# A four-layer graph network on one core: the first hop's chunks stay transposed from the join to the weights, the masked layer joins by products

## The chip, the cores and the metric

The kernel runs on one core of a Trainium2 chip. The metric is the device time of one execution in microseconds. Engines are named as the profile names them: PE (TensorE, with PEld for its weight loads), DVE (VectorE), ACT (ScalarE), POOL (GpSimd) and SP (SyncE, which issues most transfers).

## The reference, cut to what matters

`x` is 4096 x 64, `adj` 4096 x 4096, all float32. Four layers follow one another, each with a layer norm and a ReLU ahead and a residual sum behind. `norm_relu` below stands for those two steps.

```python
h = norm_relu(x)                                   # layer 0
x = x + 1.0 - 0.1 * h - 0.01 * sum(h * (adj @ h), axis=1)
h = norm_relu(x)                                   # layer 1: two hops
for k in range(2):
    h = tanh(concat([adj @ h, h], axis=1) @ W[k])
x = x + h
h = norm_relu(x)                                   # layer 2: weights by position
support = h @ weight
rank = cumsum(adj != 0, axis=1); deg = rank[:, -1:]
k = minimum(deg, 100); pos = rank - (deg - k)
x = x + where(adj != 0 and pos > 0, 0.5 ** (k - pos), 0) @ support + bias
h = norm_relu(x)                                   # layer 3
u = tanh(concat([h, t], axis=1) @ W1 + b1) @ W2 + b2
XB = h @ B.T
x = x + u + adj @ XB - sum(adj, axis=1) * XB
```

In a hop, `concat([adj @ h, h]) @ W` is computed as `adj @ (h @ Wtop) + h @ Wbottom`. The kernel keeps `h @ Wtop` in `X` as the next sweep's source and `h @ Wbottom` in `Z` until the sweep's sums are there.

## The kernel before

Five sweeps run over the whole adjacency: L0 (layer 0), L1A and L1B (the two hops), L2 (the masked layer) and L3. A sweep is 8 chunks of 512 result rows, a chunk is 16 blocks, and a block is two tiles of 128 source rows by 512 columns in float32. Two blocks, a pair of 1 MB, come with one transfer. Fifteen pairs stay in SBUF (`cache`). All others pass through six slots of `land`, in an order that turns round from sweep to sweep (L1A and L2 run backward over the chunks), so that the last six pairs of one sweep serve the next. Apart from the first chunk, a sweep loads six pairs a chunk, and seven in the one chunk that caches only one pair. SP issues the load of a slot (`load`, L714) when the instructions that read it are done: TensorE's block in all sweeps but L2, the mask on VectorE in L0 and L2 (L1116), the row totals on VectorE in L1A and L1B (L1085).

In L0, L1A, L1B and L3 a block is two products (L1320), one tile each, side by side in the two column halves of the array: 64 columns of weights (`X`), 512 columns of adjacency streaming. The two halves of the accumulator `accA` hold the sums of the even and the odd tiles, transposed (features on the partitions). So each chunk has an epilogue: ScalarE copies `accA` to `accS` (L821), and the *join* on TensorE (L1222) adds the two halves with a stacked identity, `wt("join")`. With `accS` as the weights the join also turns the chunk into rows: 4 x 2 products of 64 columns.

In L1A the epilogue goes on like this. `hop_added` on VectorE (L975) adds `Z`. ScalarE takes the tanh into `hS` (L833). The *turn* on TensorE (L1196, `transposed`) transposes four tiles, ScalarE copies them to `rowsT` (L801), and the *hop* (L1257) multiplies them with 128 columns of hop weights, which gives rows for `X` and `Z` (copied by L837). L0's epilogue ends with the same turn and hop. `rowsT` is also used, under the name `partS`, by the counting of L0's neighbours; the last step of that on VectorE is `left` (L1030), which raises `left_made`.

In L1B the tanh goes to `natS`, is added to the rows, normalized, turned and multiplied by the layer 2 weights (key 6, L1247). Its copy to `natS` is key 8 on ScalarE (L851), and GpSimd splits the result into high and low halves (`split_rows`).

In L2 the mask of a block is a step of VectorE (L1116), six blocks ahead of TensorE. TensorE multiplies the mask with a triangle (`triangle`, L1357), ScalarE turns the counts into weights (L564; in two blocks of a chunk, 3 and 13, VectorE does that, L562), and TensorE multiplies them with the rows, three blocks later (`weigh`, L1370). The result is a full 128-partition accumulator with a high and a low half of the features. Its join is four transposes of 128 x 128 (L1214), half in one block and half in the next, and VectorE adds both halves one after the other (L1054, L1057), centres the rows (L946, L947), forms the variance (L952, L953) of what GpSimd squared (L741), and after GpSimd's `pow` and scaling (L734, L744) writes the normalized rows (`norm_rows`, L965). TensorE transposes them (L1234) and multiplies them with `B.T` (L1244).

No scheduler orders the epilogues. Each engine runs through the same loop of blocks, and tables give the block behind which a step of an epilogue is put on each engine: `STAGES_L0`, `STAGES_L1A`, `STAGES_L1B`, `STAGES_L2` for a chunk's epilogue within the sweep, and `QUICK` for the last chunk's, which falls into the next sweep's chunk 0. An engine waits where it comes to a step whose input isn't there, and everything behind it on that engine waits too. On VectorE the keys of L2 count one higher than the step's number: key 4 is the sum and centring, 5 the variance, 6 the norm.

Of the kernel before, what the change touches and what calls it, by code (L numbers as in the profile page):

```python
# [17 lines left out]
D = 64  # L18
# [136 lines left out]
def copied_no(p, c, i=0):  # L155

    return {L0: c, L1B: 8 + 2 * c + i, L2: 24 + c, L3: 32 + c}[p]


def tr_no(p, c):  # L160

    return {L0: c, L1A: 8 + c, L1B: 16 + c, L2: 24 + c}[p]
# [91 lines left out]
def evac_no(c, b):  # L254
# [5 lines left out]
HT_PE = {L0: "turn", L1A: "turn", L1B: "turn", L2: 7}  # L260
HT_ACT = {L0: "turned", L1A: "turned", L1B: "turned", L2: 7}
# [6 lines left out]
STAGES_L1A = {1: 2, "added": 4, "tanh": 6, "turn": 8, "turned": 9, "hop": 11, "hopped": 13}  # L268
STAGES_L2 = {0: 2, "join0": 4, "join1": 5, 4: 5, 5: 7, 6: 9, 7: 13, 8: 15}
STAGES_L1B = {1: 3, "added": 5, "tanh": 6, 3: 7, 4: 8, 5: 10, "turn": 12, "turned": 13, 6: 15, 7: 15}  # L270
# [3 lines left out]
         L1B: {1: 1, "added": 2, "tanh": 3, "turn": 5, "turned": 5, "hop": 7, "hopped": 8},  # L274
         L2: {"tanh": 0, 4: 2, 5: 4, "turn": 8, "turned": 9, 6: 10, 7: 10, 8: 11,
# [15 lines left out]
LEFT_L1A = {"counts": 3, "weights": 4, "left": 6, "left out": 8}  # L291
# [3 lines left out]
def stages_after(p, c, b, before, before2):  # L295
# [12 lines left out]
    if p == L1B:  # L308
        found = at_block({8: 2}, before2) if before2 else []
        return found + at_block(STAGES_L1B, before) + at_block({"rows": ROWS_AT}, (p, c))  # L310
# [30 lines left out]
def gnn_kernel(nc, x_in, adj_in, left_in_d, wts_in, tri_in, out):  # L341
# [8 lines left out]
    with ExitStack() as ctx:  # L350
# [178 lines left out]
        def hop_out(i):  # L529
            return spare[:, 2:4, 0:2 * P].rearrange("p b (t y d) -> p y b t d", y=2, d=D)[:, i]  # L530
# [267 lines left out]
        def _(act):  # L798
# [4 lines left out]
            def epilogue(at, e):  # L803
# [25 lines left out]
                if at == "tanh":  # L829
# [3 lines left out]
                    nc.scalar.activation((hS if p == L1A else natS)[:, :], tS[:, :], ACT.Tanh).then_inc(tanh_done, 1)  # L833
                if at == "hopped":
                    act.wait_ge(hop_done, hop_no(p, c) + 1)
                    for of, to in ((0, X[1] if p == L0 else X[0]), (1, Z)):
                        nc.scalar.activation(chunk(to, ch(p, c)).rearrange("p (b t d) -> p b t d", b=2, d=D),  # L837
                                             hop_out(of), ACT.Copy).then_inc(hop_evac, 1)
                if at == HT_ACT.get(p, None):
# [4 lines left out]
                    if p in (L0, L1A):  # L844
                        act.wait_ge(left_made, min(c + 1, NC - 1) if p == L0 else NC)
# [84 lines left out]
        def _(dve):  # L930
# [36 lines left out]
            def epilogue(at, e):  # L967
# [64 lines left out]
                elif p in (L1B, L2):  # L1032
# [6 lines left out]
                    if at == 3:  # L1039
# [8 lines left out]
                        else:  # L1048
# [4 lines left out]
                            parts = nat_of(p, c).rearrange("p (t h d) -> p h t d", h=2, d=D)  # L1053
# [129 lines left out]
        def _(pe):  # L1183
# [22 lines left out]
            def epilogue(at, e):  # L1206
                p, c = e
                if p == L2 and at in ("join0", "join1") or p == L2 and c == NC - 1 and at == 1:
# [16 lines left out]
                if at == HT_PE.get(p, None):  # L1225

                    tr_free(tr_no(p, c))
                    if p == L1A:
                        pe.wait_ge(tanh_done, tanh_no(p, c) + 1)
                    else:  # L1230
                        pe.wait_ge(h_ready, row_no(p, c) + 1)
# [245 lines left out]
```

## Time and profile before

| | |
|---|---|
| median of 3 runs | 705.63 us (705.1 to 707.02) |
| the profiled execution | 706.86 us |
| its span | 705.1 us |
| TensorE busy | 668.3 us, 95% |
| weight loads busy | 266.6 us, 38% |
| VectorE busy | 467.3 us, 66% |
| ScalarE busy | 195.6 us, 28% |
| GpSimd busy | 113.6 us, 16% |
| HBM traffic | 366 GB/s over the span |
| the last chunk of L0, L1A, L1B is copied from accA at | 177.5, 304.0, 428.2 us |

A busy share is a mean over the five sweeps. TensorE's instructions are pipelined and overlap in the rows, so a row's busy time is longer than what the row costs: the distance between the starts of two rows is the cost. "x16" is the number of instructions in a row. What stands in brackets is how long the engine was idle before the row, and what ended that. A load's time to landing counts from its issue, so it grows with the queue ahead of it.

### The profile page before, as it was taken

Reading aid. Unit: us, or ns where it says so; the run is one execution under the profiler, and the core shown is the slowest. Engines: PE = TensorE matmul, PEld = TensorE weight load, DVE = VectorE, ACT = ScalarE, POOL = GpSimd, SP = SyncE. Lnnn points to the kernel's source line nnn. Section 1 sums busy time; section 2 is a strip of 40 time slices with the busy share of each in tenths; the row PEclk is TensorE's granted clock in tenths of the full one; section 3 lists DMA queues with packets and bytes.
Section 4 is the critical chain, followed back from the end, with each engine's and each line's share of the span. In section 5 each row is a group of like instructions: output and inputs, shape, how many; then the busy total and the mean of one; then the engine's idle time right before and its main releaser. Section 6 shows DMA issues by size and latency. Waiting matters only on the chain.

```text
span 705.1 us, 10672 instructions
## 1 busy us (share of the span) xinstructions
PE 668.3 (95%) x3920; PEld 266.6 (38%) x3920; DVE 467.3 (66%) x796; ACT 195.6 (28%) x304; POOL 113.6 (16%) x132
## 2 busy tenths in 40 slices
PE   3999999999999999999999997999999999999997
PEld 1423333333433333343443333444444433333332
DVE  7677667777899999876888778899988910000000
ACT  2101111011211111111110016888888821111110
POOL 5111011111200000001322222222222211211111
PEclk9999999999999999999999999999999999999999
DMA  9999999998699999859999985999999379999992
GB/s 356 422 413 413 416 412 413 419 415 330 212 347 391 423 421 420 367 206 399 419 417 418 415 349 192 350 381 403 415 412 410 131 243 350 420 415 412 420 416 88
DMA packets 45220, 258.64 MB, mean 367 GB/s; under 512 B 6320, under 2 KB 14256, under 8 KB 14960
## 3 DMA queue, kind: packets, MB, share of 16 engines
q1 hardware_dynamic: 39528, 252.85, 89.0%
q10 hardware_dynamic: 5640, 5.10, 2.2%
q8 instruction: 32, 0.52, 0.3%
q14 instruction: 20, 0.16, 0.1%
HBM read 253.33 MB, written 4.59 MB: 366 GB/s over the span
## 4 chain that ended last, share of the span: by engine, by line
PE 59%; DMA 20%; DVE 14%; issue 3%; POOL 2%; ACT 1%; SPq 1%; ACTq 0%; DVEq 0%
PE accA L1320 39%; DMA land<-adj_blocks 17%; PE work L1357 6%; PE accA L1370 6%; DVE uS L1085 5%; DVE uS L1116 3%; DMA cache<-adj_blocks 2%; PE work L1222 2%; PE work L1283 1%; POOL rstd L734 1%; PE work L1196 1%; DVE wS L562 1%; PE accA L1289 1%; PE work L1338 1%; PE work L1257 1%
## 5 line engine op out<-in xcount | busy, mean ns | idle before, releaser
L1320 PE MATMUL accA<-land,X 128*64 128x512 f32 x1568 | 376.1, 599 | 15.9 <-DVE X L1157 10.9
L1320 PEld LDWEIGHTS accA<-land,X 128*64 128x64 f32 x1568 | 106.1, 137 | 190.5 <-issue 157.9
L1116 DVE TENSOR_SCALAR uS<-land 128x1024 bf16<-128x1024 f32 (+1 forms) x196 | 135.2, 733 | 29.3 <-DMA land<-adj_blocks 28.3
L1085 DVE TENSOR_TENSOR uS<-uS,land 128x512 f32<-128x512 f32 x194 | 138.7, 715 | 10.5 <-DMA land<-adj_blocks 0.7
L1320 PE MATMUL accA<-cache,X 128*64 128x512 f32 x480 | 118.3, 597 | 2.9 <-ACT accS L821 2.9
L564 ACT ACTIVATE wS<-work 128x1024 uint16<-128x1024 f32 x114 | 109.0, 1035 | 14.5 <-PE work L1357 13.6
L741 POOL TENSOR_TENSOR hS<-tS 128x256 f32<-128x256 f32 x24 | 23.5, 978 | 397.6 <-DVE tS L947 397.6
L1071 DVE TENSOR_TENSOR zS<-uS,work 128x256 f32<-128x256 f32 x8 | 3.4, 421 | 122.7 <-PE work L1222 105.6
L1357 PE MATMUL work<-uS,triA 128*128 128x512 bf16 x256 | 76.0, 379 | 7.2 <-DVE wS L562 5.8
L1370 PE MATMUL accA<-wS,X 128*128 128x512 bf16 x256 | 75.8, 379 | 0.0
L821 ACT ACTIVATE accS<-accA 128x512 f32<-128x512 f32 x32 | 19.1, 596 | 155.1 <-PE accA L1320 151.6
L1320 PEld LDWEIGHTS accA<-cache,X 128*64 128x64 f32 x480 | 35.3, 138 | 63.1 <-issue 52.8
L1338 PE MATMUL work<-uS,later 128*64 128x512 bf16 x256 | 49.0, 379 | 0.0
L1116 DVE TENSOR_SCALAR uS<-cache 128x1024 bf16<-128x1024 f32 (+1 forms) x60 | 39.4, 686 | 8.0 <-DMA cache<-adj_blocks 7.8
L734 POOL TENSOR_TENSOR rstd<-var,power 128x4 f32<-128x4 f32 (+1 forms) x25 | 31.8, 1271 | 35.6 <-DVE var L953 35.6
L1370 PEld LDWEIGHTS accA<-wS,X 128*128 128x128 f16 x256 | 25.0, 98 | 30.0
L801 ACT ACTIVATE rowsT<-work 128x256 f32<-128x256 f32 x24 | 9.2, 384 | 95.4 <-PE work L1196 95.4
L1357 PEld LDWEIGHTS work<-uS,triA 128*128 128x128 bf16 x256 | 23.1, 97 | 33.4 <-issue 8.8
L1085 DVE TENSOR_TENSOR uS<-uS,cache 128x512 f32<-128x512 f32 x46 | 31.8, 691 | 2.6
L1338 PEld LDWEIGHTS work<-uS,later 128*64 128x64 bf16 x256 | 16.3, 110 | 35.6 <-issue 28.3
L965 DVE TENSOR_SCALAR hS<-tS 128x256 f32<-128x256 f32 x24 | 10.0, 416 | 27.9 <-POOL tS L744 27.9
L1222 PEld LDWEIGHTS work<-wts,accS 128*64 128x64 f32 x512 | 20.7, 138 | 17.7 <-issue 16.1
(94 smaller groups left out, 383.9 us busy)
## 6 DMA issues: line engine op xcount, KB each, us to landing
land<-adj_blocks SPq DMA_DIRECT2D x221, 1024.0 KB, 10.4
cache<-adj_blocks SPq DMA_DIRECT2D x15, 1024.0 KB, 16.6
xin<-x_rows ACTq DMA_DIRECT2D x16, 128.0 KB, 7.0
x_rows<-zS ACTq DMA_DIRECT2D x9, 128.0 KB, 7.3
out_rows<-zS ACTq DMA_DIRECT2D x8, 128.0 KB, 7.0
uS<-counts ACTq DMA_DIRECT2D x60, 4.0 KB
x_rows<-zS SPq DMA_DIRECT2D x7, 128.0 KB, 10.9
rows_transposed<-rowsT SPq DMA_DIRECT2D x7, 128.0 KB, 7.8
```

Source lines behind the costliest of these rows:

```text
L564: ops.activation(w, of, ACT.Relu).then_inc(w_ready, 1)
L734: nc.gpsimd.tensor_tensor(out[:, 0:ntile], of[:, 0:ntile], power[:, 0:ntile], ALU.pow)\
L741: nc.gpsimd.tensor_tensor(hS[:, :], tS[:, :], tS[:, :], ALU.mult).then_inc(rows_squared, 1)
L821: last = nc.scalar.activation(accS[:, :], accA[:, c % 2, :], ACT.Copy)
L965: nc.vector.tensor_scalar(to, tS[:, :], 0.0, float(np.sqrt(D)), ALU.max, ALU.mult).then_inc(h_ready, 1)
L1085: nc.vector.tensor_tensor(total, total, of[:, i * W:(i + 1) * W], ALU.add)\
L1116: nc.vector.tensor_scalar(masks(b)[0:rows, :], block_of(p, c, b)[0:rows, :], 0.0, None, ALU.not_equal)\
L1222: last = nc.tensor.matmul(nat[half, j * D:(j + 1) * D], accS[:, at:at + D], wt("join"), start=True, stop=True)
L1320: last = nc.tensor.matmul(accA[k * D:(k + 1) * D, c % 2, :], tile(X[p % 2], TQ * q + k), of[:, k * W:(k + 1) * W], start=(b == 0), stop=(b ...
L1338: last = nc.tensor.matmul(spare[k * D:(k + 1) * D, c % 2, :], later[:, NT - t:NT - t + D], masks(b)[:, k * W:(k + 1) * W], start=(b == 0), ...
L1357: last = nc.tensor.matmul(work[:, 2 * tri_pair(n) + k, :], triA[:, :], masks(b)[:, k * W:(k + 1) * W], start=True, stop=True)
L1370: last = nc.tensor.matmul(accA[:, c % 2, :], tile16(TQ * q + k), weights(n)[:, k * W:(k + 1) * W].bitcast(BF16), start=(b == 0 and k == 0) ...
```

## The change

In L0 the hop's product is made in two forms: rows for `X` as before, with the first 64 columns of the weights, and the part for `Z` transposed, by two products with 64 x 64 weights and 256 columns of `rowsT` streaming. In L1A the join streams `accS` through `wt("join")` in two products of 256 columns, which leaves the chunk transposed. `Z` is added in that form, the tanh writes `rowsT` directly, and the hop reads it. The steps `turn` and `turned` are gone from L1A. The tanh waits for the hop before it and for `left_made`, since `rowsT` is shared; the last steps of L0's counting run one block sooner (`LEFT_L1A`). In L1B the product is behind block 14 instead of 15 and its copy behind block 15 instead of block 2 of the chunk after. In L2 the join is four products with 64 columns of `wt("join")`, so that TensorE adds the halves, and VectorE has one addition instead of two. The norm is behind block 10 instead of 9, and for L1B's last chunk variance and norm are behind L2's blocks 0 and 2 instead of 2 and 4.

```diff
-STAGES_L1A = {1: 2, "added": 4, "tanh": 6, "turn": 8, "turned": 9, "hop": 11, "hopped": 13}
-STAGES_L2 = {0: 2, "join0": 4, "join1": 5, 4: 5, 5: 7, 6: 9, 7: 13, 8: 15}
-STAGES_L1B = {1: 3, "added": 5, "tanh": 6, 3: 7, 4: 8, 5: 10, "turn": 12, "turned": 13, 6: 15, 7: 15}
+STAGES_L1A = {1: 2, "added": 4, "tanh": 6, "hop": 8, "hopped": 10}
+STAGES_L2 = {0: 2, "join0": 4, "join1": 5, 4: 5, 5: 7, 6: 10, 7: 13, 8: 15}
+STAGES_L1B = {1: 3, "added": 5, "tanh": 6, 3: 7, 4: 8, 5: 10, "turn": 12, "turned": 13, 6: 14, 8: 15}
...
-         L1B: {1: 1, "added": 2, "tanh": 3, "turn": 5, "turned": 5, "hop": 7, "hopped": 8},
-         L2: {"tanh": 0, 4: 2, 5: 4, "turn": 8, "turned": 9, 6: 10, 7: 10, 8: 11,
+         L1B: {1: 1, "added": 2, "tanh": 3, "hop": 5, "hopped": 6},
+         L2: {"tanh": 0, 4: 0, 5: 2, "turn": 8, "turned": 9, 6: 10, 7: 10, 8: 11,
...
-LEFT_L1A = {"counts": 3, "weights": 4, "left": 6, "left out": 8}
+LEFT_L1A = {"counts": 2, "weights": 3, "left": 5, "left out": 7}
...
-        found = at_block({8: 2}, before2) if before2 else []
-        return found + at_block(STAGES_L1B, before) + at_block({"rows": ROWS_AT}, (p, c))
+        return at_block(STAGES_L1B, before) + at_block({"rows": ROWS_AT}, (p, c))
...
-        return [(1, before), (8, before2)]
+        return [(1, before)]
...
-        def hop_out(i):
+        def hop_out(p, i):
+            if p == L0 and i:
+                return spare[:, 2, CH:2 * CH].rearrange("p (b t d) -> p b t d", b=2, d=D)
+            if p == L0:
+                return spare[:, 2:4, 0:P].rearrange("p b (t d) -> p b t d", d=D)
...
                     if p == L1B:
                         act.wait_ge(copy_used, copied_no(p, c))
-                    nc.scalar.activation((hS if p == L1A else natS)[:, :], tS[:, :], ACT.Tanh).then_inc(tanh_done, 1)
+                    else:
+                        act.wait_ge(hop_done, hop_no(p, c))
+                        act.wait_ge(left_made, NC)
+                    nc.scalar.activation((rowsT if p == L1A else natS)[:, :], tS[:, :], ACT.Tanh).then_inc(tanh_done, 1)
...
-                            nc.vector.tensor_tensor(rows4(tS), rows4(chunk(X[0], ch(p, c))), parts[:, 0], ALU.add)\
-                                .then_inc(copy_used, 1)
-                            dve.wait_ge(copy_used, copied_no(p, c, 0) + 1)
-                            nc.vector.tensor_tensor(rows4(zS), rows4(tS), parts[:, 1], ALU.add).then_inc(nat_evac, 1)
+                            nc.vector.tensor_tensor(z, chunk(X[0], ch(p, c)), nat_of(p, c)[:, 0:CH], ALU.add)\
+                                .then_inc(nat_evac, 1)
...
-                        last = nc.tensor.transpose(nat_of(p, c)[:, j * P:(j + 1) * P], accS[:, j * P:(j + 1) * P],
-                                                   wt("ident"))
+                        last = nc.tensor.matmul(nat_of(p, c)[:, j * D:(j + 1) * D], accS[:, j * P:(j + 1) * P], wt("join"),
+                                                start=True, stop=True)
...
-                    for j, at, half in pieces(4):
-                        last = nc.tensor.matmul(nat[half, j * D:(j + 1) * D], accS[:, at:at + D], wt("join"),
-                                                start=True, stop=True)
+                    if p == L1A:
+                        for h in range(2):
+                            last = nc.tensor.matmul(nat[h * D:(h + 1) * D, 0:CH], wt("join"), accS[:, h * CH:(h + 1) * CH],
+                                                    start=True, stop=True)
+                    else:
+                        for j, at, half in pieces(4):
+                            last = nc.tensor.matmul(nat[half, j * D:(j + 1) * D], accS[:, at:at + D], wt("join"),
+                                                    start=True, stop=True)
...
-                    pe.wait_ge(tr_evac, tr_no(p, c) + 1)
+                    if p == L0:
+                        pe.wait_ge(tr_evac, tr_no(p, c) + 1)
+                    else:
+                        pe.wait_ge(tanh_done, tanh_no(p, c) + 1)
...
+                    w = D if p == L0 else P
                     for t in (0, 2, 1, 3):
                         half = (t // 2 * D, t // 2 * D + D)
-                        last = nc.tensor.matmul(spare[:, 2 + t // 2, t % 2 * P:(t % 2 + 1) * P],
+                        last = nc.tensor.matmul(spare[:, 2 + t // 2, t % 2 * w:(t % 2 + 1) * w],
                                                 rows_t(t % 2)[half[0]:half[1], :],
-                                                wt("hop0" if p == L0 else "hop1", rows=half), start=True, stop=True)
+                                                wt("hop0" if p == L0 else "hop1", 0, w, rows=half), start=True, stop=True)
+                    if p == L0:
+                        for h in range(2):
+                            half = (h * D, (h + 1) * D)
+                            last = nc.tensor.matmul(spare[half[0]:half[1], 2, CH:2 * CH], wt("hop0", D, P, rows=half),
+                                                    rowsT[half[0]:half[1], :], start=True, stop=True)
```

## Rows read from the trace of the kernel before

**Rows 1.** The chain that ended last, in order of time: start us, us, what

```profile
160.50 14.73 DMA land<-adj_blocks
...
291.58 5.15 PE accA L1320 x24
```

**Rows 2.** Timeline, ScalarE, end of L1A: start us, us, engine, line, [idle before]

```profile
288.59 0.60 ACT L821 ACTIVATE accS<-accA 128x512 f32<-128x512 f32 x1 [2.93 <-PE accA L1320]
...
304.02 0.60 ACT L821 ACTIVATE accS<-accA 128x512 f32<-128x512 f32 x1 [2.93 <-PE accA L1320]
```

**Rows 3.** Timeline, TensorE, one chunk of L1A

```profile
260.08 0.63 PE L1222 MATMUL work<-wts,accS 128*64 128x64 f32 x16
260.55 4.46 PE L1320 MATMUL accA<-land,X 128*64 128x512 f32 x20
...
265.70 0.61 PE L1196 MATMUL work<-wts,hS 128*64 128x128 f32 x8
...
266.14 1.03 PE L1320 MATMUL accA<-cache,X 128*64 128x512 f32 x4
...
268.81 0.72 PE L1257 MATMUL work<-wts,rowsT 64*128 64x128 f32 x8
```

**Rows 4.** Timeline, TensorE and VectorE, L1A's chunk 1

```profile
203.92 0.66 PE L1196 MATMUL work<-wts,hS 128*64 128x128 f32 x8 [0.73 <-ACT hS L833]
...
203.36 0.68 DVE L1030 SCALAR_TENSOR_TENSOR countS<-lowS,rowsT 32x512 uint16<-32x512 f32 x1
```

**Rows 5.** Adjacency loads by window of issue: 280, 498, 532, 535.8 us

```profile
L725 SPq DMA_DIRECT2D land<-adj_blocks x1: 327/327/327, 280.5 to 280.5; - x1
...
DMA to landing us min/median/max: 11.2/11.2/11.2
...
DMA to landing us min/median/max: 10.5/11.6/13.2
...
DMA to landing us min/median/max: 11.3/11.9/13.4
...
L725 SPq DMA_DIRECT2D land<-adj_blocks x1: 328/328/328, 535.8 to 535.8; - x1
```

**Rows 6.** By stretch: us, PE, PEld, DVE, ACT, POOL, PEclk, DMA, GB/s

```profile
290.00:305.00 15.00, 15.00 (x96) 5.79 (x94) 11.21 (x17) 2.06 (x5) 0.00 (x0) 1.00 0.50 207
```

**Rows 7.** Timeline, TensorE, a chunk of L0

```profile
154.50 1.08 PE L1320 MATMUL accA<-land,X 128*64 128x512 f32 x4 [1.14 <-DMA land<-adj_blocks]
```

**Rows 8.** Timeline, TensorE, L2's chunk 0

```profile
439.69 0.66 PE L1196 MATMUL work<-wts,hS 128*64 128x128 f32 x8 [1.15 <-DVE hS L965]
```

**Rows 9.** Timeline, TensorE, a period of L2

```profile
465.98 0.59 PE L1357 MATMUL work<-uS,triA 128*128 128x512 bf16 x2 [0.96 <-DVE wS L562]
...
470.72 0.38 PE L1214 MATMUL accA<-wts,accS 128*128 128x128 f32 x2
...
479.32 0.41 PE L1234 MATMUL accA<-wts,hS 128*128 128x128 f32 x2 [0.23 <-DVE hS L965]
...
481.30 0.61 PE L1244 MATMUL accA<-wts,rowsT 128*128 128x128 f32 x4
```

**Rows 10.** Timeline, VectorE, L2

```profile
472.32 0.42 DVE L1054 TENSOR_TENSOR tS<-X,accA 128x256 f32<-128x256 f32 x1 [0.27 <-PE accA L1214]
472.78 0.42 DVE L1057 TENSOR_TENSOR zS<-tS,accA 128x256 f32<-128x256 f32 x1
...
478.47 0.71 DVE L965 TENSOR_SCALAR hS<-tS 128x256 f32<-128x256 f32 x1 [1.00 <-POOL tS L744]
...
489.20 0.42 DVE L1054 TENSOR_TENSOR tS<-X,accA 128x256 f32<-128x256 f32 x1 [0.27 <-PE accA L1214]
...
550.19 2.48 DVE L1116 TENSOR_SCALAR uS<-land 127x1024 bf16<-127x1024 f32 x4
```

**Rows 11.** Groups by line, weight loads: count | busy us, mean ns

```profile
L1222 PEld LDWEIGHTS work<-wts,accS 128*64 128x64 f32 x512 | 20.7, 138 | 17.7 <-issue 16.1 <-ACT natS L851 1.3
...
L1244 PEld LDWEIGHTS accA<-wts,rowsT 128*128 128x128 f32 x32 | 4.7, 191 | 1.8 <-issue 0.8
```

More of the change, by code:

```diff
@@ L155, in copied_no @@
 def copied_no(p, c, i=0):
-    return {L0: c, L1B: 8 + 2 * c + i, L2: 24 + c, L3: 32 + c}[p]
+    return {L0: c, L1B: 8 + 2 * c + i}[p]
 def tr_no(p, c):
-    return {L0: c, L1A: 8 + c, L1B: 16 + c, L2: 24 + c}[p]
+    return {L0: c, L1B: 8 + c, L2: 16 + c}[p]
 TOTALS = {L1A: (1, 2, 3, 4, 7, 9, 10, 11, 12, 15), L1B: (0, 5, 6, 8, 13, 14)}
@@ L257, in evac_no @@
     return sum((k in evac_on_dve(i)) == on_dve for i in range(c + 1) for k in range(b if i == c else NQ))
-HT_PE = {L0: "turn", L1A: "turn", L1B: "turn", L2: 7}
-HT_ACT = {L0: "turned", L1A: "turned", L1B: "turned", L2: 7}
+HT_PE = {L0: "turn", L1B: "turn", L2: 7}
+HT_ACT = {L0: "turned", L1B: "turned", L2: 7}
 ROWS_AT = 12
@@ L837, in epilogue @@
                         nc.scalar.activation(chunk(to, ch(p, c)).rearrange("p (b t d) -> p b t d", b=2, d=D),
-                                             hop_out(of), ACT.Copy).then_inc(hop_evac, 1)
+                                             hop_out(p, of), ACT.Copy).then_inc(hop_evac, 1)
                 if at == HT_ACT.get(p, None):
@@ L843, in epilogue @@
                     act.wait_ge(tr_done, tr_no(p, c) + 1)
-                    if p in (L0, L1A):
-                        act.wait_ge(left_made, min(c + 1, NC - 1) if p == L0 else NC)
+                    if p == L0:
+                        act.wait_ge(left_made, min(c + 1, NC - 1))
                     rows_transposed(p, c)
@@ L1052, in epilogue @@
                             dve.wait_ge(nat_done, nat_no(p, c, 0) + 1)
-                            parts = nat_of(p, c).rearrange("p (t h d) -> p h t d", h=2, d=D)
-                            nc.vector.tensor_tensor(rows4(tS), rows4(chunk(X[0], ch(p, c))), parts[:, 0], ALU.add)\
-                                .then_inc(copy_used, 1)
-                            dve.wait_ge(copy_used, copied_no(p, c, 0) + 1)
-                            nc.vector.tensor_tensor(rows4(zS), rows4(tS), parts[:, 1], ALU.add).then_inc(nat_evac, 1)
+                            nc.vector.tensor_tensor(z, chunk(X[0], ch(p, c)), nat_of(p, c)[:, 0:CH], ALU.add)\
+                                .then_inc(nat_evac, 1)
                             dve.wait_ge(nat_evac, nat_no(p, c, 0) + 1)
@@ L1227, in epilogue @@
                     tr_free(tr_no(p, c))
[L1228 to L1231, printed above, removed]
+                    pe.wait_ge(h_ready, row_no(p, c) + 1)
                     if p == L2:
@@ L1250, in epilogue @@
                 if at == "hop":
-                    pe.wait_ge(tr_evac, tr_no(p, c) + 1)
+                    if p == L0:
+                        pe.wait_ge(tr_evac, tr_no(p, c) + 1)
+                    else:
+                        pe.wait_ge(tanh_done, tanh_no(p, c) + 1)
                     if hop_no(p, c):
                         pe.wait_ge(hop_evac, 2 * hop_no(p, c))
+                    w = D if p == L0 else P
                     for t in (0, 2, 1, 3):
                         half = (t // 2 * D, t // 2 * D + D)
-                        last = nc.tensor.matmul(spare[:, 2 + t // 2, t % 2 * P:(t % 2 + 1) * P],
+                        last = nc.tensor.matmul(spare[:, 2 + t // 2, t % 2 * w:(t % 2 + 1) * w],
                                                 rows_t(t % 2)[half[0]:half[1], :],
-                                                wt("hop0" if p == L0 else "hop1", rows=half), start=True, stop=True)
+                                                wt("hop0" if p == L0 else "hop1", 0, w, rows=half), start=True, stop=True)
+                    if p == L0:
+                        for h in range(2):
+                            half = (h * D, (h + 1) * D)
+                            last = nc.tensor.matmul(spare[half[0]:half[1], 2, CH:2 * CH], wt("hop0", D, P, rows=half),
+                                                    rowsT[half[0]:half[1], :], start=True, stop=True)
                     last.then_inc(hop_done, 1)
```

## The prediction, written before the changed kernel was run

> **What bounds the kernel now.** The page comes first: TensorE is busy nearly all the time, VectorE two thirds of it, but these are averages over five sweeps with different limits. So the next view is the chain that ended last, in order of time. The reader is to see in it that the first sweep (L0, to 178 us) is a chain of adjacency transfers, and that the first hop (L1A, to 304 us) is TensorE's own work from 204 us on [rows 1]. Behind that, the second hop (L1B, to 429) alternates between VectorE, transfers and TensorE, the masked layer (L2, to 568) between TensorE and two VectorE steps in every chunk, and the last sweep (L3) is TensorE again. So an instruction saved on TensorE counts fully in L1A, not in L0, and in L2 only as part of a loop. The timelines of single engines then give the price of each step, and the issues of the adjacency loads with their time to landing show how much lead is left.
>
> **L1A, the turn that goes.** A chunk takes 304.02 - 288.59 = 15.43 us [rows 2]. TensorE's timeline [rows 3] prices its steps. Sixteen instructions more than four cost 4.46 - 1.03, so a block of four costs 0.857 us and 0.17 of a row is the pipeline's drain. The join costs 0.63 - 0.17 = 0.46, the turn 265.70 to 266.14 = 0.44. The change deletes the turn and its copy on ScalarE. The new join streams 256 columns in the same kind of pair as a block does 512, so 0.43. The hop stays. That is 0.48 us less a chunk (with 0.01 at the changeover), and six chunks have it whole: -2.9.
>
> Chunk 1 is an exception. Its turn already waits 0.73 for the tanh [rows 4]. The new tanh writes rowsT, so it also waits for `left_made`, whose step L1030 runs on VectorE right behind `added` and takes 0.68, to 204.04 [rows 4]. A tanh of about 0.42 and a handover of 0.14 follow: the hop starts near 204.65 where TensorE is free at 203.15. Before, wait and turn together cost 0.73 + 0.46; now the wait costs 1.5, so with the join +0.2. Nobody but TensorE waits for this tanh. The eighth epilogue lies in L1B's chunk 0: -0.44. Together **-3.1 us**.
>
> Do the transfers allow it? The tightest load of the last chunk is issued at 280.5 and lands 11.2 later, at 291.7 [rows 5]. TensorE wants it in block 6, at 288.45 + 0.46 + 6 x 0.857 = 294.1. Its slack of 2.4 meets a gain there of 5 x 0.48 - 0.2 = 2.2. It just fits; up to 1 us may be lost. Behind it the transfers are busy only half of the time, and VectorE 11.21 of 15 us [rows 6]: neither holds L1B's start, which moves by what L1A gains.
>
> **L0.** Two products of 256 columns are added to the hop (half a block, 0.43) and the four old ones lose half of their columns. The old hop costs 0.72 - 0.17 = 0.55 to 0.65 [rows 3]; the new one is between +0.2 (the old ones fall with their columns) and +0.65 (weight loads show). TensorE waits 1.14 us for a load in the chunk shown [rows 7], and the chain there is a transfer: **0**. With that cover gone it is 8 x 0.65 = 5 us.
>
> **L1B.** The product and its copy to natS come one or more blocks sooner, with GpSimd's split and SP's row copies behind them. Nobody on the chain waits for them: 0, and they can't cost, as each waits for less.
>
> **The start of L2.** Variance moves from block 2 to 0, the norm from 4 to 2. TensorE's transposes of that chunk waited 1.15 us for the norm [rows 8]. Variance now goes ahead of two masks, about 0.65 each, which covers that wait. Queued behind it on VectorE: masks 7 and 8 come 0.6 later, and TensorE reaches them at about that moment. I take **-1.0**, bounds 0 and -1.15.
>
> **L2, the loop.** Its period is 489.20 - 472.32 = 16.88 us [rows 10]. TensorE's transposes (L1214) release VectorE at 472.32. VectorE does two adds, centring, masks, variance, waits 1.00 for GpSimd at L965, and four masks later comes L562, the weights for which TensorE waits 0.96, to 465.98 in the period shown [rows 9]. From there TensorE needs 6.34 us to 472.32. VectorE's part shrinks twice. One add goes: 472.32 to 472.78, 0.46. The norm moves behind one more mask (0.60), which fills 0.60 of the 1.00. Together 1.06 a loop.
>
> TensorE's part grows. Four transposes become four products, each of two instructions with 64 columns and 128 x 128 float32 weights. By the columns alone, L1222's rate (16 instructions in 0.46, side by side in pairs, so 58 ns a pair [rows 3]), 8 x 0.058 = 0.46, against 2 x (0.38 - 0.16) = 0.44 before [rows 9]: nothing. But loading weights of 64 columns takes 138 ns, of 128 columns 191 [rows 11], so 64 columns are 53 ns and 128 about 107. L1244 has the same weights and takes 0.61 - 0.17 = 0.44 for four instructions [rows 9], about 107 each. Then 8 x 0.107 = 0.86, +0.42 a chunk. I take that, as L1244 is the nearest row; the other end is 0. The Trainium skill, "TensorE: Matmul & The Clock Gate", section "LDWEIGHTS (loading the stationary operand)", says that a load of P columns takes P / 1.2 ns. By it 128 columns are 107 ns and the edit costs 0.42 us a chunk; without the rule it costs nothing. The trace's 53 ns for 64 columns agree.
>
> A loop thus gives 1.06 - 0.42 = 0.64. Six loops close before chunks 2 to 7: -3.8. The last chunk has one more join (+0.42) and loses the wait at L1234 (0.23, and its handover [rows 9]): about 0.
>
> **The second limit in L2 is the transfers.** Within two chunks, at the same places, the time to landing goes from 10.5, 11.6 and 13.2 us (least, median, most) to 11.3, 11.9 and 13.4 [rows 5]. The queue grows, so a chunk's six loads with the small ones need a little more than 16.88 us, and a shorter period only eats lead. The tightest load is issued at 535.8 and lands 13.4 later, at 549.2; its mask is the third of the four that start at 550.19 [rows 10], at 551.4. Slack 2.2. Add 0.27 that VectorE waits there for TensorE anyway (as at 489.20 [rows 10]) and about 1 us, an estimate, for what the shallower queue of the first chunks can win: 3.5. The loop wants 3.8, so I take **-3.5**. Bounds: -2.2 (lead alone) and 6 x 1.06 + 0.35 = -6.7 (products for nothing, transfers no limit).
>
> **L3.** Its chunk 0 holds the last of these joins: **+0.4**. The rest is unchanged.
>
> **Sum:** -3.1 - 1.0 - 3.5 + 0.4 = -7.2. The profiled execution took 706.86 us, 1.76 around its span of 705.1; it would take 699.7. The median of the runs, 705.63, lies 1.2 below it: **698.4 us**.
>
> **Rivals.**
> 1. The loop gets its full gain. For it: no load is late in L2 now, and L1222 is fast. Against it: [rows 5, 11]. L2 gives 6.7 and L3 nothing: 705.6 - 3.1 - 1.0 - 6.7 = 694.8; with L2's start at its best and a faster join in L1A 694.2.
> 2. Transfers bind harder: only the lead of 2.2 can be won in L2, and L1A loses 1 to landings: -2.1 - 1.0 - 2.2 + 0.4 = -4.9, 700.7; with no gain at L2's start 701.7.
> 3. Nothing that can be measured: L1B, whose chain has transfers in it too, gives back what L1A gains, and L2 keeps its period since its transfers need 17 us a chunk: 704 to 707. Against it: the idle transfers ahead of L1B [rows 6] and the lead above.
> 4. Slower. Each new small instruction pays its weight load by itself, 0.19 us [rows 11]. In L2 a join grows by 8 x 0.19 - 0.44 = 1.1, seven of them +7.6 and L3's +1.1, against 6.7 of VectorE's gain. In L1A it cancels the 0.48. L0's hop grows by 12 x 0.19 - 0.6 = 1.7, over its cover of 1.14, +4.5 in eight chunks if every chunk has only that cover, about +2 if half of them do. With -1.0 at L2's start +3.0: 708.6. It decides from about 0.15 us an instruction. Against it: in [rows 3] no small product is exposed like that.
>
> **Chances.** Forecast (696.5 to 700) 0.48; rival 1 0.20; rival 2 0.20; rival 3 0.08; rival 4 0.04. The range runs from the best end of rival 1 to the worst of rival 2, 694.2 to 701.7. A measurement of this kernel can tell about 0.3% from no change, 2.1 us: faster 0.88, within 0.3% 0.08, slower 0.04.
>
> **What would show it.** L1A's period at 14.95 us, and a hop in its chunk 1 that waits 1.5. TensorE's wait of 1.15 at L2's start gone. In L2 a period near 16.25 first, and later near 16.9 with VectorE waiting for landings; L965's wait down from 1.00 to 0.4 or less; two joins of 0.43 us each instead of 0.22. A join of 0.22, or a period under 16 that never grows, speaks for rival 1; loads that TensorE waits for in L1A for rival 2; an end of L0 that comes later for rival 4.

## The result, and the profile after

The changed kernel takes 702.28 us at the median of 15 runs (700.6 to 704.46), the kernel before 705.76 (704.41 to 709.63): ratio 0.9946, 95% interval 0.9934 to 0.9957. It is 3.5 us faster; 7.2 were forecast, and the whole range ended at 701.7, 0.6 us short. The two profiled executions flatter the change: their spans are 705.1 and 698.8 us, 6.3 apart, but the first lay 1.1 above its kernel's median and the second 1.7 below. Of the 6.3, 0.9 lies behind the last copy of `accS` (5.1 us in this trace of the kernel before, 4.2 in its second trace and in the changed kernel's), in a stretch that the change doesn't touch.

A chunk of L1A came out as forecast. TensorE, one chunk of L1A after (start us, us, engine, line):

```profile
259.34 0.60 PE L1227 MATMUL work<-accS,wts 128*64 128x256 f32 x4
259.77 4.46 PE L1335 MATMUL accA<-land,X 128*64 128x512 f32 x20
264.06 1.03 PE L1335 MATMUL accA<-cache,X 128*64 128x512 f32 x4
265.02 0.71 PE L1267 MATMUL work<-wts,rowsT 64*128 64x128 f32 x8
```

The join costs 259.34 to 259.77, 0.43, and no turn stands between the blocks. ScalarE's copies of `accS` are 14.95 us apart, where [rows 2] have 15.43:

```profile
256.99 0.60 ACT L825 ACTIVATE accS<-accA 128x512 f32<-128x512 f32 x1 [5.50 <-PE accA L1335]
271.94 0.60 ACT L825 ACTIVATE accS<-accA 128x512 f32<-128x512 f32 x1 [5.50 <-PE accA L1335]
```

But L0's last two hops run inside L1A's chunk 0, where no load covers them. TensorE there:

```profile
182.68 0.66 PE L1267 MATMUL work<-wts,rowsT 64*128 64x64 f32 x8
183.28 0.65 PE L1273 MATMUL work<-rowsT,wts 64*64 64x256 f32 x4
...
205.18 0.72 PE L1267 MATMUL work<-wts,rowsT 64*128 64x128 f32 x8 [0.42 <-ACT rowsT L840]
```

A new hop costs 0.60 + 0.58, twice the old one's 0.65 at most, and L1A's chunk 0 takes 18.62 us, where it took 17.57. TensorE is then late enough that chunk 1's hop waits 0.42 and not 1.5, so chunk 1 is 0.93 shorter. The two nearly cancel.

The masked layer gained half of what was forecast. TensorE, VectorE and GpSimd in one period of it, for [rows 9, 10]:

```profile
466.67 0.56 PE L1218 MATMUL accA<-wts,accS 128*128 128x64 f32 x4
...
475.54 0.41 PE L1240 MATMUL accA<-wts,hS 128*128 128x128 f32 x2 [0.15 <-DVE hS L972]
...
478.48 0.59 PE L1372 MATMUL work<-uS,triA 128*128 128x512 bf16 x2 [0.36 <-DVE wS L566]
```

```profile
468.62 0.42 DVE L1060 TENSOR_TENSOR zS<-X,accA 128x256 f32<-128x256 f32 x1 [0.61 <-PE accA L1218]
...
472.02 1.29 DVE L1120 TENSOR_SCALAR uS<-land 127x1024 bf16<-127x1024 f32 x2
...
474.68 0.71 DVE L972 TENSOR_SCALAR hS<-tS 128x256 f32<-128x256 f32 x1 [0.77 <-POOL tS L748]
```

```profile
472.18 1.77 POOL L738 TENSOR_TENSOR rstd<-var,power 128x4 f32<-128x4 f32 x1 [1.16 <-DVE var L960]
474.03 0.61 POOL L748 TENSOR_TENSOR tS<-tS,rstd 128x256 f32<-128x256 f32 x1
```

The period is 16.54 us (481.83 to 498.37 at ScalarE's copies) instead of 16.88. VectorE's wait for GpSimd is 0.77, not the forecast 0.4: GpSimd's power (L738, L734 before) takes 1.77 us instead of 1.40 now that three masks run beside it and not two. GpSimd before, and after in L2's last chunk, where the changed kernel too has only two masks there (the norm then waits 1.00):

```profile
476.34 1.40 POOL L734 TENSOR_TENSOR rstd<-var,power 128x4 f32<-128x4 f32 x1 [1.16 <-DVE var L953]
```

```profile
554.89 1.40 POOL L738 TENSOR_TENSOR rstd<-var,power 128x4 f32<-128x4 f32 x1 [1.16 <-DVE var L960]
```

And at the start of L2 the wait for the norm is gone, but the one behind it has grown. TensorE, the end of L2's chunk 0:

```profile
445.72 0.60 PE L1385 MATMUL accA<-wS,X 128*128 128x512 bf16 x2
448.09 0.37 PE L1393 MATMUL accA<-lowS,later 32*128 32x512 bf16 x1 [1.77 <-DMA later<-X]
```

L1393 multiplies the *left rows* (the last row of each tile, gathered into `later` by four small transfers a chunk). Before (waits by pair: us in total, times, longest):

```profile
PE accA L1378 <- DMA later<-X: 1.1, 1, 1.1
```

SyncE's issue of the last chunk's four rows, before and after:

```profile
446.68 2.40 SPq L626 DMA_DIRECT2D later<-X  x4
```

```profile
442.54 2.40 SPq L630 DMA_DIRECT2D later<-X  x4
```

Counted from L1B's last copy of `accS` (428.17 and 425.07), the issue comes 18.5 and 17.5 us later: it is 1.0 sooner. But from there to the product it took 5.1 us before and takes 5.5 after.

### The profile page after: what moved, and what is told of

It is laid out like the page before. It is cut to its first block, busy times and chain, and to the rows that moved or that the text cites. A ratio compares the mean times of both kernels' runs of the same rounds, so it can differ in the third digit from the quotient of the medians.

```text
span 698.8 us, 10456 instructions
## 1 busy us (share of the span) xinstructions
PE 669.3 (96%) x3824; PEld 266.5 (38%) x3824; DVE 462.8 (66%) x788; ACT 193.3 (28%) x296; POOL 113.9 (16%) x132
## 4 chain that ended last, share of the span: by engine, by line
PE 64%; DMA 20%; DVE 9%; issue 2%; POOL 1%; SPq 1%; ACT 1%; DVEq 0%; ACTq 0%
PE accA L1335 44%; DMA cache<-adj_blocks 10%; DMA land<-adj_blocks 9%; PE work L1372 6%; PE accA L1385 6%; DVE uS L1120 3%; DVE uS L1089 2%; PE work L1298 1%; PE work L1353 1%; PE work L1231 1%; PE accA L1304 1%; DVE wS L566 1%; PE accA L1218 1%; PE work L1267 1%; PE work L1200 1%
## 5 line engine op out<-in xcount | busy, mean ns | idle before, releaser
L1335 PEld LDWEIGHTS accA<-land,X 128*64 128x64 f32 x1568 | 107.5, 137 | 198.4 <-issue 167.2
L1089 DVE TENSOR_TENSOR uS<-uS,land 128x512 f32<-128x512 f32 x194 | 137.1, 707 | 10.7 <-DMA land<-adj_blocks 0.8
L1335 PE MATMUL accA<-cache,X 128*64 128x512 f32 x480 | 120.0, 600 | 2.9 <-ACT accS L825 2.9
L738 POOL TENSOR_TENSOR rstd<-var,power 128x4 f32<-128x4 f32 (+1 forms) x25 | 34.0, 1360 | 34.7 <-DVE var L960 34.7
L805 ACT ACTIVATE rowsT<-work 128x256 f32<-128x256 f32 x16 | 6.1, 383 | 72.2 <-PE work L1200 72.2
L758 POOL TENSOR_TENSOR uS<-X,rowsum 128x256 f32<-128x256 f32 x8 | 4.9, 612 | 100.3 <-DMA xin<-x_rows 78.1
```

The lines of the kernel that those rows point to most:

```text
L738: nc.gpsimd.tensor_tensor(out[:, 0:ntile], of[:, 0:ntile], power[:, 0:ntile], ALU.pow)\
L1089: nc.vector.tensor_tensor(total, total, of[:, i * W:(i + 1) * W], ALU.add)\
L1335: last = nc.tensor.matmul(accA[k * D:(k + 1) * D, c % 2, :], tile(X[p % 2], TQ * q + k), of[:, k * W:(k + 1) * W], start=(b == 0), stop=(b ...
```

## The experiments

My first theory, A: the adjacency loads take back a part of the gain, in waits that this pair of profiles shows only in part. Its rival B: the gain was never there, and the pair's 6.3 us are luck in stretches that the change doesn't touch. Times are medians, each beside runs of the kernel before on the same chip (705.98 to 706.25). "Chunk" is the distance between ScalarE's copies of `accS`.

**after_again, before_again.** The two kernels once more, no edit.

> The changed kernel once more. Its trace adds up to 5.4 us less than the one before at the last join, the timed runs to 3.5. Theory A (an ordinary execution has slower transfers than the profiled one, and the change shortens only what lies beside them): a second trace that is slower than the first shows the difference as waits for adjacency loads in L1B, L1A or L2, while L1A's steps between loads keep their period of 14.96 us and TensorE's steps their prices. Theory B (the difference is luck of the pair, in stretches that the change doesn't touch): the slower trace loses in L0 or ahead of the first block, and L1A to L3 take what they took. Both expect 0.993 to 0.997 of the time before.

> The kernel before once more, for a second trace. Theory A: waits for loads in L1B as in the first (1.2 us), none in L1A and L2; its span differs from the first mostly in L0. Theory B: the same, and the spread between the two traces of the kernel before is as wide as between the two of the changed one.

702.22 (ratio 0.9952, 0.9933 to 0.9971) and 705.4 us, spans 702.1 and 703.6: here the spans are 1.5 apart. Where nothing is late, L1A's and L2's inner chunks are the same to 0.01 us as in the first pair. The two traces of the changed kernel are 3.3 us apart at the last copy: 0.35 at L0's end, 0.65 in L1A's chunks 5 and 6, nothing over L1B as a whole (chunk 4 has +0.58, and the two behind it make it good), and 2.34 in L2's chunks 0 and 1. In the last, the granted clock had fallen. The wait for the left rows is 2.6 us in after_again, and only 0.4 in before_again.

**l1a_only, l2_only.** Only the first hop's part with L0's hop, and only the masked layer's part with VectorE's order.

> Only the transposed first hop: L0's hop in two forms, L1A's join, tanh and hop without the turn, the earlier end of L0's counting. L1B and L2 as in the kernel before. By the steps in the trace: chunks of L1A 15.43 to 14.96, six of them and L1B's chunk 0, against +1.05 for two longer hops in L1A's chunk 0 of which 0.7 remains behind chunk 1: -2.9 us. Theory A: -1.5 to -2.2 in timed runs, as L1B's transfers take the rest. Theory B: -2.9.

> Only the rest of the change: L1B's product one block sooner, the order at L2's start, L2's join by products with one addition, its norm one block later. L0 and L1A as before. By the steps in the trace: -1.0 at L2's start, six loops of 16.54 instead of 16.88 (-2.0), +0.44 in L3's chunk 0: -2.6 us. The forecast had -4.1 for these. Theory A: -1.5 to -2.6, Theory B: -2.6.

704.7 (0.9982, 0.9966 to 0.9999) and 704.82 (0.9975, 0.9955 to 0.9996), so -1.3 and -1.2 where the forecast had -3.1 and -4.1, and the expectations -2.9 and -2.6. Each part does its chunks as in the changed kernel (14.96, and 16.54), and each falls short elsewhere. In l1a_only TensorE and VectorE wait for loads in L1A's middle chunks (chunk 3 takes 16.92). In the four traces of the old order with full loads TensorE's products don't wait there; VectorE's rows do, 0.7 to 2.3 us in all, and up to 0.5 us of it shows in the chunks. Waits by pair, L1A, l1a_only:

```profile
DVE uS L1093 <- DMA land<-adj_blocks: 3.1, 10, 0.6
PE accA L1339 <- DMA land<-adj_blocks: 1.3, 3, 0.6
```

In l2_only the wait for the left rows is 2.8 us. TensorE there, and the stretches around it (us; busy PE, PEld, DVE, ACT, POOL; clock, DMA share, GB/s):

```profile
448.51 0.59 PE L1366 MATMUL accA<-wS,X 128*128 128x512 bf16 x2
451.93 0.58 PE L1374 MATMUL accA<-lowS,later 32*128 32x512 bf16 x1 [2.83 <-DMA later<-X]
452.45 0.61 PE L1353 MATMUL work<-uS,triA 128*128 128x512 bf16 x1
453.28 1.06 PE L1366 MATMUL accA<-wS,X 128*128 128x512 bf16 x2 [0.22 <-ACT accS L818]
```

```profile
445.00:450.00 5.00, 4.11 (x19) 1.35 (x16) 4.30 (x6) 4.83 (x6) 1.34 (x2) 1.00 0.87 310
450.00:455.00 5.00, 2.84 (x7) 0.99 (x9) 1.48 (x2) 0.60 (x1) 0.00 (x0) 0.69 0.95 370
455.00:460.00 5.00, 5.00 (x28) 2.86 (x27) 3.35 (x7) 4.19 (x5) 1.00 (x1) 0.97 1.00 367
```

A pair of products takes 1.06 instead of 0.59 for 3.4 us behind the wait: the clock has gone from 2.4 to 1.2 GHz, and L2's chunk 1 takes 18.19 us where the changed kernel's takes 16.80. Every trace in which the clock falls here has a mean clock of 0.998 or less, and every other 0.999 or 1. By that mark the clock fell in 8 of l2_only's 12 executions, whose median is 705.6; that of the other four is 702.5. So most of what this part misses goes with the clock. In the changed kernel it fell in 4 of 22. This gave theory C: the gain of L2's new start is spent in the wait for the left rows, at times with the clock.

**one_left.** The left rows of a chunk by one transfer.

```
-                for t in range(4 * c, 4 * c + 4):
-                    sp.dma_start(loS[t:t + 1, :], tile16(t)[LAST:P, :]).then_inc(left_rows, 16)
+                four = X[1][LAST:P, 4 * c * D:(4 * c + 4) * D].bitcast(F16)
+                sp.dma_start(loS[4 * c:4 * c + 4, :], four.rearrange("o (t w) -> o t w", t=4)).then_inc(left_rows, 16)
```

> The changed kernel, with the four left rows of a chunk sent by one transfer instead of four. SyncE spends 2.4 us on the four of the last chunk of masked layer 1's second half, so its last row should land up to 1.8 us earlier. Three traces of the new order at layer 2's start show TensorE standing 1.8, 2.6 and 2.8 us for those rows ahead of L1393; in the first the granted clock stayed at 1.00, in the other two it read 0.69 in the 5 us behind the wait, and chunks 0 and 1 of layer 2 took some 2.4 us longer together. Theory C (the gain of the new start is spent in this wait, and the clock's fall behind it costs more than the wait itself): wait under 1 us, clock 1.00 in every run, median 1.0 to 2.5 us under the changed kernel's 702.3, so 700 to 701. Theory A (the missing gain is lost to adjacency loads in many places): the wait shrinks, the median falls by 0.5 us at most. Rival: one transfer of four rows from one partition lands no earlier, since what takes its time is the way behind the adjacency loads; wait 1.8 or more, median 702 to 703.

700.69 us (0.9921, 0.99 to 0.9942), 1.6 less than the changed kernel. SyncE spends 0.60 on the rows of the last chunk; the wait is 1.3 us (not under 1), and no execution had a mean clock under 0.999. Theory C's number is met, theory A's 0.5 is not. The Trainium skill, "DMA: Bandwidth & Descriptors", section "Rules for kernel authors", says to coalesce many small transfers into one large one; here four of 256 bytes against one are worth 1.6 us, together with the clock that doesn't fall.

**old_start.** L2's start in the old order.

```
-STAGES_L1B = {... 5: 10, "turn": 12, "turned": 13, 6: 14, 8: 15}
+STAGES_L1B = {... 5: 10, "turn": 12, "turned": 13, 6: 15, 7: 15}
-         L2: {"tanh": 0, 4: 0, 5: 2, ...
+         L2: {"tanh": 0, 4: 2, 5: 4, ...
-        return [(1, before)]
+        return [(1, before), (8, before2)]
```

> The changed kernel with the order of work at layer 2's start, and of the last masked layer 1 chunks' norm, as before (normalized rows two blocks later, turn in block 12, its product in block 15 of the chunk ahead); the joins by products stay. By my prediction's term for that order (-1.0) this is 1.0 us slower than the changed kernel: 703.3. Theory C: the wait for the left rows goes back to 1.1 us and the clock stays at 1.00, so it is no slower, and at the median as fast or up to 1 us faster: 701.5 to 702.5. Theory A: 703.3 as by the term.

701.99 us (0.9946, 0.9928 to 0.9963): not slower, where my term of -1.0 for the new order asks for 703.3. The wait for the left rows is 0.8 us, and no execution has a mean clock under 0.999. The traces show what cancels: from L1B's last copy to L2's chunk 1 this one takes 40.57 us, the new order 40.22 where the clock holds and 42.56 where it falls.

**old_join.** The two joins by transposes again, with VectorE's two adds.

> The changed kernel, with layer 2's and layer 3's join back to eight transposes (two of each kind of tile) and, in layer 2, VectorE's two adds. My terms: TensorE 0.34 a chunk less in the join (0.44 instead of 0.78), VectorE 0.46 more; in the trace of the changed kernel the loop of layer 2 is bound by TensorE and its waits (16.54 a chunk), so without the products the chunk is 16.4 to 16.7, and layer 3's first chunk is 0.44 shorter. Sum over six chunks and layer 3: 702.3 within 1 us either way. If VectorE's second add was the whole gain, the chunk returns to 16.88: +2 us in the loop less 0.44, 704.

704.06 us (0.9966, 0.9952 to 0.9981): the total expected if the chunk went back to 16.88, but it doesn't. Its inner chunks take 16.65, so the products win 0.11 a chunk; L3's chunk 0 is 0.44 shorter. The two nearly cancel. The rest of its distance lies where the edit changes nothing: the left rows' wait (2.5 us in its trace, the clock at 0.66 behind it) and 1.9 us in L1A's chunks 3 and 4 with waits for loads. The clock fell in 7 of its 12 executions; the other five have a median of 702.8, and the changed kernel's without a fall 702.1. Why it fell so often here isn't known. As an answer on the total it is unclear; on the chunk it is clear.

**norm_at_11.** Norm and turn in L2 one block later.

```
-STAGES_L2 = {... 5: 7, 6: 10, 7: 13, 8: 15}
+STAGES_L2 = {... 5: 7, 6: 11, 7: 14, 8: 15}
```

> The changed kernel, with VectorE's normalization in layer 2 one block later (11) and the product behind the turn one block later too (14). In the trace of the changed kernel VectorE waits 0.77 us for GpSimd's power ahead of it, and TensorE then 0.36 for wS behind. One mask more (0.60) covers most of that wait. Theory B of the loop (VectorE's wait is what the loop still pays): chunk 16.54 to about 16.1, six chunks 2.5 us faster: 700. Theory A (adjacency loads need about 17 us a chunk once the slots' slack is used up; the tightest load had 1.2 us left in the changed kernel): the first two or three chunks gain, later ones wait for landings; 0.5 to 1.5 us faster in all. Rival: TensorE is the loop's bound by then, and the later rows make it wait for the turn instead: no change, 702 to 703.

701.71 us (0.9938, 0.9916 to 0.996), chunks of 16.28 and not 16.1. That should give 1.4 us in all (the last chunk is 0.2 longer); the median shows 0.5, in seven executions of which the clock fell in three. No instruction waits for an adjacency load in L2 behind chunk 0. GpSimd and VectorE there:

```profile
474.40 1.77 POOL L738 TENSOR_TENSOR rstd<-var,power 128x4 f32<-128x4 f32 x1 [1.16 <-DVE var L960]
476.25 0.95 POOL L748 TENSOR_TENSOR tS<-tS,rstd 128x256 f32<-128x256 f32 x1
```

```profile
477.24 0.71 DVE L972 TENSOR_SCALAR hS<-tS 128x256 f32<-128x256 f32 x1 [0.51 <-POOL tS L748]
```

One mask more fills 0.60, and the scaling beside it now takes 0.95 instead of 0.61: 0.60 - 0.34 = 0.26, the gain of the chunk. Every trace with the norm in block 10 or 11 has the power at 1.77 in the chunks before the last and at 1.40 in the last, where two masks stand beside it; every one with the norm in block 9 has 1.40 throughout.

**rows_late.** The kernel before, with three small transfers that nothing reads ahead of the last left rows.

> The kernel before, with three more small transfers (of 256 bytes, into memory that nothing reads) in SyncE's queue ahead of the last four left rows, so that these land some 1.8 us later (3 x 0.6 us of SyncE). In layer 2's chunk 0 TensorE should then stand about 2.9 us for the left rows instead of 1.1. Theory C (a wait of 2.5 us or more at this place lets the granted clock fall, whatever the rest of the kernel): in most runs the clock reads about 0.7 in the 5 us behind the wait and the mean clock of the run is 0.997 to 0.998; the median rises by the 1.8 us and by another 1 to 1.5 us, so 708.5 to 709.5. Rival: the fall belongs to the new order of work at layer 2's start and not to the wait; then the clock stays at 1.00 and the median is 707.5 to 708.

706.68 us against 706.25 (1.0005, 0.9991 to 1.0019): no change that can be told from none, where 708.5 to 709.5 (C) or 707.5 to 708 was expected. The wait grew by 0.7, to 1.78, and not to 2.9: the three transfers took 1.04 us of SyncE and not 1.8, and the last row landed 2.4 us after its issue instead of 3.3. In its profiled execution the clock fell all the same (0.80 and 0.86 in the two stretches of 5 us behind the wait), and one other of the twelve has the same mean clock, 0.997. So the fall is not tied to the new order; five of the some 60 executions of the kernel before have such a mean too, though where their clock fell no trace shows. Nor does the length of the wait alone decide: 2.5 us in norm_at_11's trace left the clock at 1.00.

**one_left_norm_at_11.** Both edits.

> The changed kernel with both edits: the left rows of a chunk by one transfer, and layer 2's normalization and the product behind the turn one block later. Alone they gave 1.6 us (700.69 against 702.3) and, in the loop of layer 2, 16.28 instead of 16.54 a chunk, with 701.71 at the median in spite of a wait of 2.5 us for the left rows. Theory C, where the two are independent: 700.7 less 6 x 0.26, so 699 to 699.5, and the clock at 1.00 in nearly all runs. Theory A: adjacency loads give back what the loop gains, 700.5 or more.

699.03 us (0.9895, 0.9877 to 0.9912): 3.2 less than the changed kernel, the best version, and theory C's number (699 to 699.5; theory A had 700.5 or more). The left rows' wait is 0.6. In L2's chunk 6 the loads bind, 16.78 instead of 16.28. VectorE:

```profile
544.14 1.30 DVE L1120 TENSOR_SCALAR uS<-land 127x1024 bf16<-127x1024 f32 x2 [0.89 <-DMA land<-adj_blocks]
```

**before_light, after_light.** Both kernels, each adjacency load behind L0 cut to three quarters: the last quarter of each pair is left out, so these two kernels don't compute the reference.

```
-                sp.dma_start(land[:, slot, :], rows_of(p, c, k)).then_inc(landed[slot], 16)
+                kept = PAIR if p == L0 else PAIR * 3 // 4
+                sp.dma_start(land[:, slot, 0:kept], rows_of(p, c, k)[:, 0:kept]).then_inc(landed[slot], 16)
```

> The kernel before, in which every adjacency load behind layer 0 moves only the first three quarters of its pair of blocks; the last quarter of each pair is left out. It keeps every instruction, and shows the kernel with loads that are never late. Expected from its two traces, where TensorE stood 1.2 and 0.7 us for adjacency loads in layer 1's second half and 1.1 us for the left rows: 1 to 3 us faster than the kernel before, 703 to 705. It is the partner of the changed kernel with the same loads.

> The changed kernel, with the same three quarters of each adjacency pair behind layer 0 (the rest is left out). Theory A (loads eat about 1 us in chunks 3 to 5 of masked layer 1's first half, where five of seven traces with the new order wait for them and none of the old, and some more behind): the distance to the kernel before with the same loads grows from 3.5 us to the sum of the terms that the traces show without waits: 3.2 in masked layer 1, 6 x 0.34 in layer 2, less 0.44 in layer 3, so 4.8 to 5.8 us. Theory C alone: the left rows land sooner too, so the clock stays at 1.00 and the distance grows to 4.5. Were neither loads nor rows the cause, it stays at 3.5.

703.62 and 697.48 us: 6.1 apart, where the full loads leave 3.5. Theory A had 4.8 to 5.8, theory C alone 4.5. The loads' last quarter costs the kernel before 2.6 us and the changed one 4.8. Theory B is out as the main cause: the gain is there, and 2.6 us of it are given back. This pair alone can't part A from C, since the left rows too land sooner beside lighter loads; the stretches can.

Where it is given back, from the copies of `accS` (us; full loads: the mean of all traces that have the order of the stretch in question, old and new, rows_late left out where its own edit lies):

| stretch | forecast | light pair | full loads |
|---|---|---|---|
| L0's last copy to L1B's first | -3.1 | 141.98 to 138.79, -3.2 | 142.26 (4 traces) to 139.80 (8), -2.5 |
| L1B | 0 | 107.14 to 106.40, -0.7 | 108.00 (5) to 108.08 (7), +0.1 |
| L1B's last to L2's chunk 1 | -1.6 | 40.01 to 39.21, -0.8 | 40.95 (3) to 41.89 (3), +0.9 |
| L2's chunk 1 to its last | -2.9 | 98.63 to 96.86, -1.8 | 98.64 to 96.85, -1.8 |
| L2's last to L3's first | +0.4 | +0.4 | +0.4 |
| sum | -7.2 | -6.1 | -2.8 |

The light pair's sum agrees with its medians. The full loads' is 0.7 short of theirs, and the third row says why: in two of its three new traces the clock had fallen (42.56 and 42.89), but in the changed kernel's executions only 4 times in 22. The trace in which it held has 40.22, that is -0.7, nearly what the light pair has. So the third row's loss against the light pair goes with the fallen clock. The first two rows' losses are loads. Single traces of one order differ by 1 to 3 us in each of the three upper rows, so the full loads' sum is not good to better than some tenths. (Sums are of unrounded figures.) TensorE, waits for loads in L1B's trace after:

```profile
373.48 1.08 PE L1335 MATMUL accA<-land,X 128*64 128x512 f32 x4 [0.70 <-DMA land<-adj_blocks]
...
404.55 1.08 PE L1335 MATMUL accA<-land,X 128*64 128x512 f32 x4 [0.44 <-DMA land<-adj_blocks]
```

TensorE's products wait 1.4 and 1.1 us in L1B in the two traces of the changed kernel, 1.2 and 0.7 in those of the kernel before, and not at all in the light pair.

## Why the prediction was wrong

**What bounds the kernel.** Right for L0, L1A and L2's loop. Of the 3.7 us missing, three steps cost most, told below: one term of L2's loop (1.5 us), L2's start (0.6, and 2.3 to 2.7 more where the clock falls) and the cover of the loads in L1A (0.7). The last is a failed reading: I saw the transfers busy half of 290 to 305 us [rows 6] and asked only the last chunk's load whether L1A may be shorter. A mean over 15 us says nothing of the loads of chunks 3 to 6.

**L1A, -3.1.** The mechanism and the chunk (14.95) were right, and without late loads the stretch gives -3.2. "It just fits; up to 1 us may be lost" was asked of the last chunk's load [rows 5]; the loss of 0.7 came, but in chunks 3 to 6. The forecast should have looked for the tightest load of every chunk.

**L0: 0** left out that two of its hops run in L1A's chunk 0. The 1.05 us they cost there were paid by chunk 1's wait, which I had priced at 1.5 (+0.2 in all; measured +0.12). Two errors cancelled, which is luck. The new hop, 1.18 against 0.55 to 0.65, lies near the upper bound that I allowed (+0.65): halving the columns of the eight old instructions saved 0.05, and the four new ones of 256 columns cost 0.58, not half a block's 0.43. L0's end itself comes 0.4 us later, 177.65 to 178.01 (means of five and nine traces), with single traces up to 1.2 apart: a loss that I put at 0 and that these traces can't settle.

**L1B: 0** was right by luck: its new order gives -0.7 where loads are light (chunks of 15.07 instead of 15.21), and loads take it back.

**L2's start, -1.0.** The failed step is "TensorE reaches them at about that moment": I named the two masks behind the moved steps and did not ask what TensorE waits for next. That is the left rows. Counted from L1B's last copy, TensorE comes to them 1.3 us sooner (21.25 instead of 22.54), and SyncE issues them 1.0 sooner, but they are there 5.5 to 6.6 us after the issue (five traces) instead of 4.4 to 5.2 (four). A wait of 0.4 to 1.1 became one of 1.8 to 2.8. Why they take longer isn't shown; the two adjacency loads ahead of them in SyncE's queue are issued 4.3 us before them instead of 5.2, so a queue behind these loads is likely. Even with light loads, where the clock holds, the wait of 1.16 that goes leaves one of 0.76 here: the third row's -0.8 is -0.34 of the loop and -0.5 of the start, half of my term.

**L2's loop, -3.5.** Mis-sized term: VectorE's 1.06 was 0.69. The add gave its 0.46. The masks gave not 0.60 but 0.60 - 0.37 = 0.23, as GpSimd's power beside them went from 1.40 to 1.77 us. The changed kernel's own last chunk, with two masks, has 1.40 and a wait of 1.00 again. TensorE's join was right: two halves of four instructions at 0.39, 0.78 against 0.44, +0.34 (forecast +0.42). 0.69 - 0.34 = 0.35, and the chunk shows 0.34. Six loops give 2.0 us, not 3.5. By the same figures old_join must lose 0.46 - 0.34 = 0.12 (it loses 0.11) and norm_at_11 win 0.26 (it does). The rule of the Trainium skill, "TensorE: Matmul & The Clock Gate", section "LDWEIGHTS (loading the stationary operand)", P / 1.2 ns, gives 107 ns an instruction. The rows show 98 (0.39 over four), within a tenth of that and far from the 58 by columns: the rule held. Without it the loop's term would have been larger by another 0.42 a chunk.

**The second limit, transfers in L2** at 3.5 us: not refuted and not reached. The loop wanted only 2.0. At 16.28 a chunk they bind in chunk 6 of one_left_norm_at_11 and nowhere in norm_at_11, so the lead was about what [rows 5] said or more.

**L3, +0.4:** measured 0.44.

**The rivals.** The outcome lies past rival 2 and is part of its mechanism, transfers that bind, but in L1 and at L2's start and not in L2's loop. Its 700.7 to 701.7 took L1A's loss rightly; its -2.2 for the loop is close to the 2.0 measured, but by luck: it is the loads' lead, and what held the loop was GpSimd and TensorE's join. It had no larger wait at the start and no clock. Rival 4 was wrong where it counted: a small product of the join costs 0.098 us, not 0.19.

## What to carry to other kernels

Before a wait is taken out of a chain, follow the engine to the next thing that it waits for, and ask whether that lands earlier too, and not only whether it is issued earlier; here at least half of 1.0 us moved from one wait to the next. A step put beside a GpSimd operation is not free cover: subtract what GpSimd gets slower by. And check the lead of the loads in each chunk, not in the last: with lighter loads the same change gave 6.1 us, with the real ones 3.5.

## What the runs showed of the hardware

- GpSimd's `pow` of 128 x 4 took 1.40 us where VectorE's masks ended 0.27 before it, and 1.77 where masks ran to within 0.04 of its end or past it; its scaling of 128 x 256 took 0.61 with VectorE idle and 0.95 beside a mask. The Trainium skill, "GPSIMD Engine Reference", section "1. Specifications", has GpSimd's way to SBUF shared with VectorE, with contention when VectorE's instruction is in a 2-port mode or reads two inputs from SBUF. A slowing beside masks agrees with that; whether the masks were in such a mode no run shows.
- The granted clock fell from 2.4 to 1.2 GHz for 3.4 us behind an idle stretch of TensorE of 2.5, 2.6 and 2.8 us (old_join, after_again, l2_only) and of 1.8 (rows_late); it stayed behind 1.8 in a fifth trace (after) and 2.5 in a sixth (norm_at_11). With the left rows in one transfer, or with light loads, no mean clock of 20 executions is under 0.999. What decides between the six stays open.
- Four rows of 256 bytes in one transfer were there 4.4 and 5.1 us after the start of their issue (one_left_norm_at_11, one_left), beside the adjacency loads; in four transfers 5.5 to 6.6 us after the start of the first one's in the five traces with the new order of L2's start, and 4.4 to 5.2 in four with the old one.
